# Attention scores as one plain 32-bit product instead of three products of halves

## The reference

```
q = einsum('bmd,ed->bme', x, w_q)          k, v alike
q_rot = _rotate(q, cos, sin)               k_rot alike
scores = einsum('bqd,bkd->bqk', q_rot, k_rot) / sqrt(128)
scores = where(causal, scores, -inf)
out = einsum('bqk,bkd->bqd', softmax(scores), v)
```

## Time and profile before

| | |
|---|---|
| median of 3 timed runs | 840.92 us (840.55 to 841.94) |
| span of the profiled execution | 839.7 us |
| PE busy | 828.4 us, 99% of the span |
| DVE busy | 726.4 us, 87% |
| POOL busy | 612.6 us, 73% |
| ACT busy | 527.4 us, 63% |
| granted TensorE clock, mean | 0.999 |

### The profile page before, as it was taken

One profiled execution on the slowest core, in us unless ns is written; L12 is line 12 of the kernel. 1 busy time (PEld: TensorE's weight loads), 2 busy tenths in 40 slices (PEclk: granted clock), 3 DMA queues, 4 the chain that ended last, 5 costly groups with the idle time before them and its releaser, 6 DMA issues.

```text
span 839.7 us, 16434 instructions
## 1 busy us (share of the span) xinstructions
PE 828.4 (99%) x4374; PEld 692.1 (82%) x4374; DVE 726.4 (87%) x2120; ACT 527.4 (63%) x1051; POOL 612.6 (73%) x559
## 2 busy tenths in 40 slices
PE   8899999999999999999999999999999999999998
PEld 7687888888888877888999999788888888888887
DVE  7889999889998988788888877799999999998886
ACT  5556566566655677776667666566656656666564
POOL 6777777777777678888888882567777777777664
PEclk9999999999999999999999999999999999999999
DMA  5787756666776544443333430566666555555553
GB/s 188 214 252 204 187 169 171 171 174 180 186 179 176 157 99 102 127 117 99 89 103 99 126 101 2 134 165 159 155 160 162 146 155 140 140 154 142 146 147 85
DMA packets 69377, 123.09 MB, mean 147 GB/s; under 512 B 8784, under 2 KB 19904, under 8 KB 69056
## 3 DMA queue, kind: packets, MB, share of 16 engines
q1 hardware_dynamic: 69312, 122.33, 55.0%
HBM read 104.28 MB, written 9.63 MB: 136 GB/s over the span
## 4 chain that ended last, share of the span: by engine, by line
PE 58%; DVE 2%; DMA 1%; issue 1%; SPq 0%; ACT 0%; DVEq 0%; ACTq 0%
PE bank L1623 53%; PE bank L1981 4%; PE bank L1743 1%; DMA qkT<-comb_rows 1%; SPq L409 0%; DVE xl L1467 0%; DVE probT L1193 0%; PE bank L1727 0%; DVE bank L1500 0%; DMA comb_rows<-combT 0%; DVE prob L1183 0%; DVE bank L1488 0%; DVE marked L1149 0%; DVE rope_c L1473 0%; DVE stage L1477 0%
## 5 line engine op out<-in xcount | busy, mean ns | idle before, releaser
L531 POOL TENSOR_TENSOR h_l<-probT,h_h 128x512 fp32r<-128x512 f32 x254 | 329.3, 1298 | 172.8 <-ACT h_h L753 172.4
L753 ACT ACTIVATE h_h<-probT 128x512 fp32r<-128x512 f32 (+1 forms) x285 | 178.9, 628 | 83.6 <-DVE probT L1193 81.3
L1623 PE MATMUL bank<-xh,w_h 128*128 128x512 f32 x545 | 220.3, 404 | 2.2 <-DVE prob L1183 2.0
L806 ACT ACTIVATE bank<-bank 128x512 f32<-128x512 f32 x252 | 146.8, 583 | 115.3 <-PE bank L1623 115.0
L1623 PE MATMUL bank<-xh,w_l 128*128 128x512 f32 x545 | 215.0, 394 | 0.0
L1623 PE MATMUL bank<-xl,w_h 128*128 128x512 f32 x545 | 214.7, 394 | 0.0
L1183 DVE TENSOR_TENSOR prob<-bank,qkT 128x512 f32<-128x512 f32 x252 | 172.8, 686 | 33.1 <-ACT bank L806 25.7
L1193 DVE TENSOR_TENSOR probT<-prob,bank 128x512 f32<-128x512 f32 x255 | 173.9, 682 | 18.6 <-POOL h_l L531 4.5
L1623 PEld LDWEIGHTS bank<-xh,w_h 128*128 128x128 f32 x545 | 102.4, 188 | 26.5 <-DVE prob L1183 3.1
L1623 PEld LDWEIGHTS bank<-xh,w_l 128*128 128x128 f32 x545 | 102.2, 188 | 23.8
L1623 PEld LDWEIGHTS bank<-xl,w_h 128*128 128x128 f32 x545 | 102.6, 188 | 21.0
(11 more groups left out here) (137 smaller groups left out, 1334.9 us busy)
## 6 DMA issues: line engine op xcount, KB each, us to landing
qkT<-comb_rows SPq DMA_DIRECT2D x190, 256.0 KB, 5.5
qkT<-comb_rows SPq DMA_DIRECT2D x124, 128.0 KB, 3.0
rows<-comb_rows SPq DMA_DIRECT2D x28, 512.0 KB, 7.2
stage<-stage SPq DMA_DIRECT2D x64, 128.0 KB, 2.7
X<-in_x SPq DMA_DIRECT2D x16, 256.0 KB, 7.2
stage<-in_x_t SPq DMA_DIRECT2D x16, 256.0 KB, 7.6
x_t<-stage SPq DMA_DIRECT2D x16, 256.0 KB, 2.0
out_x_t<-stage SPq DMA_DIRECT2D x15, 256.0 KB, 2.0
```

Of the source, the lines that this page charges most:

```text
L531: nc.gpsimd.tensor_tensor(lo, f, hi.bitcast(F32), ALU.subtract).then_inc(done, 1)
L753: return nc.scalar.activation(dst, src, ACT.Copy)
L806: nc.scalar.activation(bank[:, G_BANK[g], :], bank[:, G_BANK[g], :], ACT.Silu).then_inc(silu_done, 1)
L1623: return nc.tensor.matmul(dst, lhsT, rhs, start=start, stop=stop)
```

## The change

The three matmuls per chunk of scores become one on plain 32-bit operands. The buffers `rot` are gone: POOL's add writes the rotated block into the first half of `qkT[p]`, now of plain 32-bit type; the second half is no longer used in the attention. ACT's high copies and POOL's low halves are gone, with their semaphores; PE waits for the adds (`rot_done`) instead of the low halves. The add of block 0 waits, from the second batch on, for the first scores of the batch before, and the adds no longer wait for low halves.

```diff
@@ buffers
-        rot = [sb(f"rot{p}", [P, TILE]) for p in range(ROPE_BUFS)]
-        qkT = [sb(f"qkT{p}", [P, 2, 2, M], F32R) for p in range(2)]
-        qkT_h = [qkT[p][:, 0, :, :] for p in range(2)]
-        qkT_l = [qkT[p][:, 1, :, :] for p in range(2)]
+        qkT = [sb(f"qkT{p}", [P, 2, 2, M]) for p in range(2)]
+        qk_rot = [qkT[p][:, 0, :, :] for p in range(2)]
@@ POOL
-            def rope_add(b, n):
+            def rope_add(b, p, n):
...
-                wait(pool, qkT_l_done, QK * b + n - ROPE_BUFS + 1)
-                nc.gpsimd.tensor_tensor(rot[s][:], rope_c[s][:], rope_s[s][:], ALU.add).then_inc(rot_done, 1)
-
-            def rope_low(b, p, n):
-
-                pool.wait_ge(qkT_h_done, QK * b + n + 1)
-                low_half(qkT_l[p][:, qk_part(n), qk_cols(n)], rot[n % ROPE_BUFS][:], qkT_h[p][:, qk_part(n), qk_cols(n)],
-                         qkT_l_done)
+                if n == 0 and not (isinstance(b, int) and b == 0):
+                    pool.wait_ge(scores_ready, QB * (b - 1) + 1)
+                nc.gpsimd.tensor_tensor(qk_rot[p][:, qk_part(n), qk_cols(n)], rope_c[s][:], rope_s[s][:],
+                                        ALU.add).then_inc(rot_done, 1)
...
                 rope_sin(b, 1)
-                rope_add(b, 1)
-                rope_low(b, p, 0)
-                rope_low(b, p, 1)
+                rope_add(b, p, 1)
...
                     attn_pack(b + 2)
-                rope_low(b, p, 2)
-                rope_low(b, p, 3)
@@ ACT
-            def attn_hi(n, b, p):
-
-                act.wait_ge(rot_done, QK * b + n + 1)
-                copy(qkT_h[p][:, qk_part(n), qk_cols(n)], rot[n % ROPE_BUFS][:]).then_inc(qkT_h_done, 1)
...
-                    if i in HI_STEP and not last:
-                        attn_hi(HI_STEP[i], b + 1, 1 - p)
@@ PE
             def attn_scores(b, p, i):
                 s = i % 2
 
-                pe.wait_ge(qkT_l_done, QK * b + 2 * (i // NB) + 2)
+                pe.wait_ge(rot_done, QK * b + 2 * (i // NB) + 2)
...
-                    ins = mm3(dst, qkT_h[p][:, 0, qs], qkT_l[p][:, 0, qs], qkT_h[p][:, 1, k0:k1], qkT_l[p][:, 1, k0:k1])
+                    ins = mm(dst, qk_rot[p][:, 0, qs], qk_rot[p][:, 1, k0:k1], True, True)
```

## The result

The changed kernel takes 846.99 us (median of 4 runs, 846.36 to 847.41), the kernel before 841.09 on the same occasions. The ratio is 1.0064, 95% interval 1.0052 to 1.0077: slower by 0.6%. The span of the profiled execution is 845.6 us, 5.9 more than before.

The account below looks back on a forecast made before the run. PE was taken to bound the kernel, busy 24.01 of 24.10 us per attention batch. Span 839.7, +10.1 for scores, -2.2 for pauses, +1.2 from span to timed median: 848.8 us, range 844.8 to 853.5.

Parts of the forecast that it names:

- The price: PE's score runs in attention: plain products at 0.222 us per 128 columns, +1.26 us per batch, +10.1 over 8 batches.
- The second way: Score price cross-check: 4 x 0.107 plus fp32r's 0.02 us excess makes 0.448 per 512-column record, twice 0.222.
- The old price: Attention scores as three fp32r products per chunk, 12 chunks: 6.74 us per batch.
- The first rival: Score runs: plain columns stream as fast as fp32r, -2.2 us per batch, -18 in all, 820.7 us; 8%.
- Four fp32r products: Score runs: a plain product costs as much as four fp32r ones, +14 us, 852.7 us; 14%.
- The relief counts for more: Attention: all PE pauses and the small restarts go, price at its lower bound, 844.8 us; 14%.
- No pause goes: POOL's work moves beside other DVE operations and slows those, so no PE pause is saved, 851.0 us; 12%.
- Pause 1: Batch 0, row 4: PE's wait for POOL's last low half goes, about 0.45 us.
- Pause 2: End of first FFN: PE's wait for POOL's low half of h shrinks 0.35 us; bounds 0 and 0.56.
- Pause 3: Row 0 of seven steady batches: PE's wait for the probT copy shrinks 0.2 us each, 1.4 in all.
- The sum: Whole run: +10.1 us for scores, -2.2 for pauses, on a span of 839.7 gives 847.6.
- The steady batch: Attention: a steady batch of about 25.1 us, POOL busy some 15 us of it, ACT 14.

Follow-up runs that it names:

- experiment 4: The changed kernel with each plain score product issued twice, the second overwriting the first; 905.25 us, 58.3 above the changed kernel.
- price_only: The kernel before with one plain product per chunk, ACT's copies and POOL's subtractions still made; 847.28 us, ratio 1.0078.
- relief_only: The changed kernel with three fp32r products per chunk, all on the rounded rotated block, low halves left out; 839.65 us, ratio 0.9986.
- pool_kept: The changed kernel with POOL's subtraction still made (block minus itself, PE waits for it), ACT's copies gone; 846.66 us, ratio 1.0076.
- act_kept: The kernel with the plain product and ACT's full-precision copy of each rotated block still made, POOL's subtractions gone; 846.77 us, ratio 1.0070.

## Why the prediction was right, and where its steps were not

- **The sign and the main mechanism: right.** PE carries the attention, the plain product costs four passes, and the time went to the runs of scores. Forecast 848.8 (844.8 to 853.5), measured 846.99. The price was put a little too high and the pauses 1.3 us too low; both errors make the forecast too high, so it was not their cancelling that kept it in the range.
- **The price: nearly right, 0.09 us per batch too large.** Forecast +1.26 us per batch at 0.222 per 128 columns; measured +1.17 (6.74 to 7.91). The step that was off is the 0.222 itself, taken from records of 128 columns and carried over to wide ones. The record of 512 columns takes 0.430, near 4 x 0.107, the lower bound from the earlier trace rows, and not 4 x 0.111; the run of two 512-column chunks took 1.72 us for the forecast 1.85. The second way failed with it: the surcharge of 0.02 us per instruction that I carried over from fp32r is next to none on the plain record. The 0.111 of a 128-column record fits the spacing that the earlier trace rows shows whatever the width, but no run separates its weight load from its columns. A plain batch of scores adds 7.7 us (experiment 4), where I had 8.0. The old price was too high as well: 7.7 less the 1.17 is 6.6 us for my 6.74, as the narrow chunks were read with their early starts. These two errors partly cancel. Over 8 batches this term is +9.4 us for the forecast +10.1.
- **The first rival (as fast as fp32r): wrong.** The run of two 512-column chunks would have taken 1.0 us and took 1.72. The rule of four passes in the Trainium skill ("FP8 and Floating Point Precision", TensorE Precision Notes) agrees with the trace: a product is two records, each 0.430 us for 512 columns, which is 2 x 512 columns at 2.4 GHz (0.427). The halved rate of the Trainium skill ("Perfetto Trace Analysis", Engine Utilization) holds per record.
- **The other rivals: wrong.** Four fp32r products would have made a chunk of 512 cost 0.93 us; it cost 0.86. "The relief counts for more" has nearly the size of the pauses (3.5 of its 3.8 us) but not the cause: in a steady batch the relief gave nothing. "No pause goes" fails by the same 3.5 us.
- **Pause 1 (batch 0, row 4): right.** Forecast 0.45 us, measured 0.53 between price_only and the changed kernel in that batch. The run started at 342.28 after a wait; now it follows its predecessor (0.05 after the start of the last v product):

```profile
342.13 0.22 PE L1593 MATMUL bank<-wqkv,xl 128*128 128x128 f32 x1
342.18 1.29 PE L1593 MATMUL bank<-qkT 128*128 128x512 f32 x4
```

- **Pause 2 (end of the first FFN), 0.35 us: wrong.** The wait named there did shrink, from 0.56 to 0.23 us. The next one, for DVE's low half, grew from 0.63 to 0.84. First the changed kernel's two weight loads:

```profile
328.90 0.19 PEld L1593 LDWEIGHTS bank<-h_h,w_h 128*128 128x128 f32 x1 [0.23 <-POOL h_l L525]
...
330.97 0.19 PEld L1593 LDWEIGHTS bank<-h_h,w_h 128*128 128x128 f32 x1 [0.84 <-DVE h_l L1033]
```

and the second one of before:

```profile
330.77 0.19 PEld L1623 LDWEIGHTS bank<-h_h,w_h 128*128 128x128 f32 x1 [0.63 <-DVE h_l L1063]
```

  The same pair of numbers returns in both kernels without ACT's copies (0.25 and 0.82 in relief_only and pool_kept) and the old pair in both with them (0.56, and 0.63 or 0.62, in price_only and act_kept), so it is the copy's doing, and it moves the wait. Of the 0.33 us that the first wait lost, the next took 0.21. I had asked what becomes early and not what is late next.
- **Pause 3 (row 0): wrong in cause, half in size.** I put the gain at up to 0.2 us per batch from the relief and 0.1 from the longer scores, and counted 0.2; measured 0.39, close to my upper bound. Only about a third of it lies at row 0's first product with v; that the v products also had pauses I had not seen. The forecast sign is there: after the scores of row 2, two records of 0.32 from 411.40, PE waited 0.13 us for the copy (until 412.17), and the scale is short. But price_only reaches the same batch with ACT and POOL at their old work. The longer scores cover the pauses by themselves. That the count came near is luck: its main term, the relief, was nothing in a steady batch. Where PE keeps its old price, in relief_only, the relief is worth 0.7 and 0.3 us in the first two batches between marks and about 0.1 in three others, and the last is 0.3 longer.
- **The sum.** Forecast +10.1 - 2.2 = +7.9; measured +9.4 - 3.5 = +5.9. Of the 3.5, 3.0 lie between the first mark and the last: 0.9 in the first interval, with the wait of batch 0, 0.6 in the second, and 0.35 to 0.39 in each of the four others. The remaining 0.5 lies outside the marks and was not taken apart; it is no more than two runs of one kernel differ by.
- **The steady batch.** Forecast 25.1 us, measured 24.84; POOL's 15 and ACT's 14 us of busy time were 14.6 and 14.9.

## What to carry to other kernels

- In these traces three fp32r products of halves are cheaper on PE than one plain 32-bit product for 512, 384 and 256 columns (0.70 for 0.86 us at 512) and dearer at 128 (0.34 for 0.22 to 0.28), where an fp32r product takes 0.11 us as it does at 16 columns. Taking work off ACT and POOL in exchange is worth only what PE waits for them.
- An engine at 99% busy with pauses of 0.1 to 0.3 us between runs sits in a loop with others: work added to it first fills the pauses (here 0.39 of 1.17 us per batch), work taken from it does not all come back (3.2 of 5.5), and a pause removed by reordering returns at the next wait. Ask of every pause what is late next.
- Test a two-sided change by its two one-sided kernels. Here the price alone reproduced the steady batch of the whole change, and that corrected a cause that the profile alone had seemed to show.

## What I had not expected of the hardware

A plain 32-bit record costs 0.430 us for 512 columns and an fp32r one 0.233, more than half of it: the surcharge over bare columns that the fp32r product shows does not appear in the plain one. And four kernels that differ by up to 5 us of POOL's work and 2.5 us of ACT's per batch have the same steady batch to 0.01 us (24.84 us on average over the last two between marks in the changed kernel, in price_only and in pool_kept, 24.85 in act_kept), and over the last four to 0.01 us as well (24.87 to 24.88).
